# A recommender tower with a three-layer cross network: another opening order, and a later copy of the third chunk's x

## Chip, cores and metric

One core of a Trainium2 chip runs the whole program. The metric is device time in microseconds (us), the median over the runs of one kernel. TensorE is called PE here, VectorE DVE, ScalarE ACT, GpSimd POOL and SyncE SP, as in the profile.

## What is computed

A batch of 512 samples, each with 64 categorical fields. Every field's row (16 floats) is gathered from its table, the 64 x 16 block x goes through three layers of a cross network, and a small multi-layer perceptron follows.

```python
e = stack([tbl_f[ids[:, f]] for f in range(64)], axis=1)     # 512 x 64 x 16
h = x = e
outs = []
for W in (W0, W1, W2):                                       # W0: 64*64 x 128, W1, W2: 64*128 x 128
    h = einsum('bid,bjd,ijn->bnd', x, h, W)
    outs.append(h)
z = sum(concatenate(outs, axis=1), axis=-1)                  # 512 x 384
h = relu(concatenate([z, dense_ctx], 1) @ W_top1 + b_top1)
h = relu(h @ W_top2 + b_top2)
y = h @ W_top3
```

## The kernel before, in words

The 512 samples x 16 dimensions are 8192 columns, worked in 16 **chunks** of 512 columns (32 samples), t = 0 to 15. All five instruction streams are written out by hand with semaphores; each runs the function `chunk(bt, q, t)` once per chunk, chunk 0 with q = -1 and the others with q = 0 to 3 in four blocks. Inside a chunk the order is given by 64 **places** p: at each place PE fills one PSUM bank of a ring of four (`fill_bank`, L848: three 128x512 matmuls, L870 to L872, for four fields i of layer 1), and either ACT (`scale_bank`, L673, at the places of `A_IN`, 7 of each 16) or DVE (`take_bank`, L551, at the other 9) takes the bank, scaling it with x and summing. PE may fill place p only when place p - 4 has been taken (L861 to L867). POOL adds up what ACT has scaled (`add_pairs`, L434, lines L447 to L453) and closes each quarter of a chunk (`finish_block`, L455). ACT may write its y buffer again only when POOL has read it (L684).

While chunk t runs, the same streams prepare the next ones at fixed places. POOL gathers the table rows of chunk t + 2 (`gather`, L422, one indirect DMA per step), SP stores them to DRAM turned (L307), loads them as x (L330, tile `xx`) and in nine rotated groups (`load_roll`, L316, tile `roll`, a ring of four). ACT copies x into the PSUM tile `xx_ps` (`copy_xx`, L631). DVE multiplies every rotated group with `xx_ps` (`product`, L501, line L519), and PE contracts these products with W0 into `acc` (layer 0, L828, L812 to L817, L823). ACT and DVE round and split the result h1 for the next chunk (L657, L540). During chunk t DVE forms the products of chunk t + 1; from chunk 1 on the first of them stands at place 0, ahead of that place's bank. ACT's copy of the x of chunk t + 2 stands at place `XX_COPY_AT` = 56 of 64 of chunk t, in chunk 0 as in all others (L762).

**The opening.** Chunk 0 is cut into two halves of 256 columns, so that layer 1 can begin with the first.
- SP loads the first indices and row offsets (L332, L333), then the other chunks' (L334, L335). POOL adds them (L486) and gathers, 8 indirect DMAs for the first half and 8 for the second (L491), then 16 for chunk 1 (L429).
- ACT issues at once, waiting for nothing, W0 in four loads (L713 to L716), three constants (L718) and W1 in eight parts of 512 KB (L720); it rounds parts 0 to 3 (L724) and waits for the first x.
- SP waits for the first 8 gathers, stores the half twice (L313, tensor `x_halves`), waits for that, loads x (L339) and the nine rotated groups, two loads each (L327). Groups 4 to 8 wait until product g - 4 has freed their ring slot. After group 3 it waits for the second half's gathers and stores that half.
- ACT copies the first x to `xx_ps` (L729), the turned x to `xcol` (L731), rounds W1's parts 4 to 7 and the split part of W0 (`w0_hi`, L736).
- DVE sums W0 (L575 to L577), forms the low parts of W1 0 to 3 (`w1_rest`, L578, line L580), then the nine products of the first half with the other four `w1_rest` after products 1, 3, 5 and 7 (L585 to L588), then the split of h1 (L546, L548) and the low part of W0 (L591).
- PE runs `WARM` = 20 matmuls on W1's first part (L919), turns the first x (L844), does layer 0 of the first half (L925), and starts `fill_bank` of chunk 0 when h1 is rounded (L739) and split (L546). The second half's layer 0 stands at places 8 to 24 of chunk 0.

```python
for g in range(GROUPS):                                         # SP, L340
    if g >= ROLL:
        sp.wait_ge(first_prod_ready, g - ROLL + 1)
    load_roll(x_halves[0], g, (g - GROUPS) % ROLL, first_roll_loaded, HALVES[0])
    if g == ROLL - 1:
        sp.wait_ge(first_gathered[1], 16 * HALF_STEPS)
        store_half(1)
```

Of the kernel before, what the change touches and what calls it, by code (L numbers as in the profile page):

```python
# [5 lines left out]
F32 = mybir.dt.float32  # L6
# [3 lines left out]
ALU = mybir.AluOpType  # L10
# [31 lines left out]
GROUPS = 9  # L42
# [6 lines left out]
W1_PARTS = 8  # L49
# [28 lines left out]
WARM = 20  # L78
# [7 lines left out]
FIRST_STORE_AT, FIRST_XX_LOAD_AT = 48, 50  # L86
# [43 lines left out]
def build(nc, ins, out):  # L130
    with ExitStack() as ctx:
# [160 lines left out]
        def gathers(t):  # L292
            return not isinstance(t, int) or t + 2 < CHUNKS
# [7 lines left out]

        @block.sync
        def _(sp):
# [6 lines left out]
            def store_half(half):  # L310
                for copy in range(2):
                    dst = x_halves[half, copy * FIELDS:(copy + 1) * FIELDS, :]
                    sp.dma_start(dst.rearrange("(s f) (b d) -> (f b) s d", f=HALF_F, d=DIM),  # L313
                                 rows[:, 0, half * HALF_STEPS:(half + 1) * HALF_STEPS, :]).then_inc(first_stored[half], 16)

            def load_roll(x, g, slot, loaded, cols=slice(0, CH)):  # L316

                width = cols.stop - cols.start
                if g == WHOLE:
                    for part in (slice(0, FIELDS // 2), slice(FIELDS // 2, FIELDS)):  # L320
                        src = x[FIELDS // 2 + part.start:FIELDS // 2 + part.stop, :]
                        sp.dma_start(roll[part, slot, 0, cols], src).then_inc(loaded[slot], 16)
                    return
                for half in range(2):
                    first = x[4 * g + half:4 * g + half + 1, :]
                    src = bass.AP(first.tensor, first.offset, [[width, FIELDS], [2 * width, 2], [1, width]])
                    sp.dma_start(roll[half * FIELDS:(half + 1) * FIELDS, slot, :, cols], src).then_inc(loaded[slot], 16)  # L327
# [12 lines left out]
            for g in range(GROUPS):  # L340
                if g >= ROLL:
                    sp.wait_ge(first_prod_ready, g - ROLL + 1)
                load_roll(x_halves[0], g, (g - GROUPS) % ROLL, first_roll_loaded, HALVES[0])
                if g == ROLL - 1:
                    sp.wait_ge(first_gathered[1], 16 * HALF_STEPS)
                    store_half(1)
# [153 lines left out]
        def _(dve):  # L500
# [81 lines left out]

            for k in range(W1_PARTS // 2):
                w1_rest(k)
            for g in range(GROUPS):  # L585
                first_product(g)
                if g % 2 == 1:
                    w1_rest(W1_PARTS // 2 + g // 2)  # L588
            first_split_h1()
            dve.wait_ge(w0_hi_ready, 1)  # L590
            dve.tensor_tensor(w0_lo[:], w0_whole[:], w0_hi[:].bitcast(F32), ALU.subtract).then_inc(w0_lo_ready, 1)  # L591
# [38 lines left out]
        def _(act):  # L630
# [81 lines left out]
            act.sem_inc(z3_copied, 1)  # L712
            act.dma_start(w0[:], ins["w0_tiles"][:, 0:RAW_TILES, :]).then_inc(w0_loaded, 16)  # L713
# [5 lines left out]
            for k in range(W1_PARTS):  # L719
                act.dma_start(w1_whole[:, w1_parts[k]], ins["w1_rows"][:, w1_parts[k]]).then_inc(w1_loaded[k], 16)  # L720

# [3 lines left out]

            for k in range(W1_PARTS // 2):
                round_w1(k)
            act.wait_ge(first_xx_loaded, 16)
# [4 lines left out]
            for k in range(W1_PARTS // 2, W1_PARTS):  # L733
                round_w1(k)
            act.wait_ge(w0_summed, 1)
            act.activation(w0_hi[:], w0_whole[:], ACT.Copy).then_inc(w0_hi_ready, 1)  # L736
# [4 lines left out]
            def chunk(bt, q, t):  # L741
                last = is_last(t)
                for p in range(PLACES):
# [18 lines left out]
                    if p == XX_COPY_AT and gathers(t):  # L762
                        copy_xx(t + 2)
# [287 lines left out]
```

## Time and profile before

| what | value |
|---|---|
| median of 3 runs | 1139.14 us (1136.38 to 1140.77) |
| the profiled execution's own time | 1139.9 us |
| its span, first to last instruction | 1138.1 us |
| PE busy | 1100.9 us (97%) |
| DVE / ACT / POOL busy | 901.2 (79%) / 684.9 (60%) / 913.9 us (80%) |
| mean granted clock of PE | 0.99 |

The span is 1.8 us short of the execution's own time. The shares are means over the whole span: what a stage loses has to be read in the stage, by the waits and the order of time there. Times in the rows further down are us from the start of the span. In the timeline a row gives start, duration, engine, line, operation and tiles, a count, and in brackets the idle time of the engine before it with what ended it; "SPq" and "ACTq" are the issuing of DMAs by SP and ACT.

### The profile page before, as it was taken

The numbers are of one execution on the slowest core, as the hardware profiler recorded it, in microseconds if no ns is written. First come the engines' busy times: TensorE is split into PE (matmuls) and PEld (weight loads), VectorE is DVE, ScalarE is ACT, GpSimd is POOL, SyncE is SP. The second block draws the span as 40 slices with busy tenths as digits, with TensorE's granted clock in tenths as the row PEclk, the third lists the DMA queues.
The fourth block names the chain that finished last, engine by engine and source line by source line (L and its number), as shares of the span: only waits on it lengthen the run. The fifth ranks groups of instructions, "written<-read, shape, count | busy, mean of one in ns | idle before, by whom it ended". The sixth has DMA issues, their size and how long they took to land.

```text
span 1138.1 us, 17464 instructions
## 1 busy us (share of the span) xinstructions
PE 1100.9 (97%) x4802; PEld 818.8 (72%) x4802; DVE 901.2 (79%) x2567; ACT 684.9 (60%) x2132; POOL 913.9 (80%) x848
## 2 busy tenths in 40 slices
PE   2898999999999999999999999999999999999999
PEld 2666677777778777777678777777777777777775
DVE  2788788988887788888887698989887588988750
ACT  3354666666664566666665466766665466666751
POOL 6778798989989598898889689898988769966740
PEclk8899899999999999999999999999999999999999
DMA  7573514252444425243251634315153621523000
GB/s 267 132 182 66 140 34 112 46 119 57 94 119 103 104 45 113 64 92 85 39 134 48 164 82 85 87 18 140 28 131 82 164 63 29 129 79 127 1 1 1
DMA packets 128100, 102.51 MB, mean 90 GB/s; under 512 B 77569, under 2 KB 87041, under 8 KB 127490
## 3 DMA queue, kind: packets, MB, share of 16 engines
q1 hardware_dynamic: 117714, 92.89, 33.0%
q0 software_dynamic: 8192, 2.11, 2.2%
q10 hardware_dynamic: 2096, 6.40, 1.4%
q8 instruction: 38, 0.62, 0.2%
q14 instruction: 60, 0.49, 0.2%
HBM read 97.16 MB, written 4.20 MB: 89 GB/s over the span
## 4 chain that ended last, share of the span: by engine, by line
PE 80%; POOL 12%; DMA 3%; issue 2%; DVE 1%; ACT 1%; SPq 0%; POOLq 0%; ACTq 0%; DVEq 0%
PE tps L870 19%; PE tps L872 18%; PE tps L871 18%; PE acc L828 8%; POOL ysum_sb L450 5%; PE side L897 5%; POOL rows_sb L429 4%; PE side L884 3%; PE acc L812 2%; PE acc L817 2%; PE acc L813 2%; PE acc L823 1%; PE side L892 1%; PE tps L964 1%; POOL ysum_sb L447 1%
## 5 line engine op out<-in xcount | busy, mean ns | idle before, releaser
L688 ACT ACTIVATE y_sb<-tps,xcol_sb 128x128 f32<-128x128 f32 x1792 | 511.5, 375 | 365.2 <-PE tps L872 325.4
L571 DVE SCALAR_TENSOR_TENSOR parts_sb<-tps,xcol_sb,parts_sb 128x128 f32<-128x128 f32 x2176 | 604.9, 341 | 152.1 <-PE tps L872 150.4
L450 POOL TENSOR_TENSOR ysum_sb<-ysum_sb,y_sb 128x512 f32<-128x512 f32 x319 | 421.0, 1320 | 72.7 <-ACT y_sb L688 50.0
L870 PE MATMUL tps<-w_hi_sb,h_hi_sb 128*128 128x512 f32 x1024 | 464.8, 454 | 6.2 <-ACT y_sb L688 4.6
L871 PE MATMUL tps<-w_lo_sb,h_hi_sb 128*128 128x512 f32 x1024 | 405.9, 396 | 0.0
L872 PE MATMUL tps<-w_hi_sb,h_lo_sb 128*128 128x512 f32 x1024 | 405.9, 396 | 0.0
L429 POOL DMA_INDIRECT rows_sb<-tables,rows_now_sb x240 | 255.4, 1064 | 61.4 <-issue 25.5
L870 PEld LDWEIGHTS tps<-w_hi_sb,h_hi_sb 128*128 128x128 f32 x1024 | 193.4, 189 | 97.2 <-issue 25.7
L871 PEld LDWEIGHTS tps<-w_lo_sb,h_hi_sb 128*128 128x128 f32 x1024 | 193.8, 189 | 65.6 <-issue 28.8
L872 PEld LDWEIGHTS tps<-w_hi_sb,h_lo_sb 128*128 128x128 f32 x1024 | 193.4, 189 | 46.6
L519 DVE TENSOR_TENSOR prod_sb<-roll_sb,xx_ps 128x1024 f32<-128x1024 f32 (+1 forms) x136 | 155.9, 1146 | 14.1 <-DMA roll_sb<-x_halves 12.7
L828 PE MATMUL acc<-prod_sb,w_sb 128*128 128x512 f32 (+1 forms) x272 | 135.4, 585 | 4.5 <-DVE prod_sb L519 4.5
L447 POOL TENSOR_TENSOR ysum_sb<-y_sb 128x512 f32<-128x512 f32 x64 | 82.6, 1291 | 17.3 <-ACT y_sb L688 8.7
L533 DVE TENSOR_TENSOR lo_sb<-prod_sb,hi_sb 128x1024 fp32r<-128x1024 f32 x60 | 95.2, 1587 | 0.3
L652 ACT ACTIVATE hi_sb<-prod_sb 128x1024 fp32r<-128x1024 f32 x60 | 64.4, 1073 | 15.6 <-DVE prod_sb L519 15.6
L699 ACT ACTIVATE gsum_sb<-side 128x256 f32<-128x256 f32 x128 | 65.1, 691 | 3.7 <-PE side L884 3.7
L828 PEld LDWEIGHTS acc<-prod_sb,w_sb 128*128 128x128 f32 x272 | 49.8, 193 | 20.6 <-issue 7.4
L453 POOL TENSOR_TENSOR ysum_sb<-ysum_sb 128x256 f32<-128x256 f32 x63 | 51.0, 810 | 4.9
L460 POOL TENSOR_TENSOR ysum_sb<-ysum_sb,parts_sb 128x256 f32<-128x256 f32 x63 | 47.7, 757 | 5.9 <-DVE parts_sb L571 0.4
L812 PE MATMUL acc<-hi_sb,w_hi_sb 128*128 128x512 f32 x120 | 48.9, 408 | 0.0
L567 DVE TENSOR_SCALAR parts_sb<-tps,xcol_sb 128x128 f32<-128x128 f32 x128 | 38.5, 342 | 11.8 <-PE tps L872 11.0
L813 PE MATMUL acc<-hi_sb,w_lo_sb 128*128 128x512 f32 x120 | 47.2, 393 | 0.0
(72 smaller groups left out, 607.6 us busy)
## 6 DMA issues: line engine op xcount, KB each, us to landing
roll_sb<-x_scratch SPq DMA_DIRECT2D x240, 256.0 KB, 4.2
w_sb<-w_rows SPq DMA_DIRECT2D x40, 256.0 KB, 4.2
gsum_sb<-w_rows ACTq DMA_DIRECT2D x8, 512.0 KB, 8.9
roll_sb<-x_halves SPq DMA_DIRECT2D x32, 128.0 KB, 2.9
rows_sb<-tables,rows_now_sb POOLq DMA_INDIRECT x240
x_scratch<-rows_sb SPq DMA_DIRECT2D x30, 128.0 KB, 4.1
xx_sb<-x_scratch SPq DMA_DIRECT2D x15, 256.0 KB
roll_sb<-x_scratch SPq DMA_DIRECT2D x30, 64.0 KB, 1.9
```

Of the source, the lines that this page charges most:

```text
L429: pool.indirect_dma_start(rows[:, slot, s, :], None, ins["tables"], bass.IndirectOffsetOnAxis(ap=rows_now[:, s:s + 1].bitcast(U32), axis=0 ...
L447: pool.tensor_tensor(ysum[:], y[:, 0], y[:, 1], ALU.add).then_inc(y_step, 1)
L450: pool.tensor_tensor(ysum[:], ysum[:], y[:, bank], ALU.add).then_inc(y_step, 1)
L519: dve.tensor_tensor(prod[:, slot, :, cols], roll[:, ring, :, cols], xx_ps[:, :, cols].to_broadcast([P, 2, cols.stop - cols.start]), ALU.mu ...
L533: dve.tensor_tensor(lo[:, slot], prod[:, slot], hi[:].bitcast(F32), ALU.subtract).then_inc(lo_ready, 1)
L571: dve.scalar_tensor_tensor(part, bank, scale, part, ALU.mult, ALU.add).then_inc(d_done, 1)
L688: done = act.activation(y[:, bank, u * NF:(u + 1) * NF], tps[:, p % RING, u * NF:(u + 1) * NF], ACT.Copy, scale=xcol[:, (q + 1) % 2, s, i: ...
L812: pe.matmul(acc[:], w0_hi[:, 2 * e + i, :], hi[:, i, :], start=False, stop=False, skip_group_check=True)
L828: mm = pe.matmul(acc[:, cols], weights, prod[:, slot, i, cols], start=g == 0 and i == 0, stop=False, skip_group_check=True)
L870: pe.matmul(bank, h1_hi[:, par, cols], w1_hi[:, of], start=True, stop=False, skip_group_check=True)
L871: pe.matmul(bank, h1_hi[:, par, cols], w1_lo[:, of], start=False, stop=False, skip_group_check=True)
L872: pe.matmul(bank, h1_lo[:, par, cols], w1_hi[:, of], start=False, stop=True, skip_group_check=True).then_inc(t_ready, 1)
```

## The change

- ACT waits for the first indices (`first_ids_loaded`) before it issues its loads of W0, constants and W1, and issues only the first four parts of W1 then.
- ACT rounds the split part of W0 right after W1's parts 0 to 3, and DVE forms its low part right after `w1_rest(3)`, ahead of the first product.
- When the first half is stored, ACT issues the second half-load of the rotated groups 0 to 3, then W1's parts 4 to 7, and then copies x and the turned x. SP issues x, the first half-load of groups 0 to 3 and both of groups 4 to 8.
- SP's store of the second half moves from after group 3 to after group 8.
- DVE's `w1_rest` of parts 4 and 5 stand after products 4 and 6, those of parts 6 and 7 after the split of h1.
- `WARM` is 26 in place of 20.
- In chunk 0 alone, ACT's copy of chunk 2's x stands at place 63 in place of 56.

```diff
--- before.py
+++ after.py
@@ -46,7 +46,8 @@
 RAW = tuple(g for g in range(WHOLE) if g not in SPLIT)
 SPLIT_TILES, RAW_TILES = 2 * len(SPLIT), 2 * len(RAW)
 ROLL = 4
-W1_PARTS = 8
+W1_PARTS, W1_EARLY = 8, 4
+W1_BEHIND = (4, 6)
 W2_I, W2_SLOTS = 4, 4
 F_SETS = FIELDS // W2_I
 W2_KEPT = 4
@@ -75,7 +76,7 @@
 HALVES = (slice(0, HALF), slice(HALF, CH))
 HALF_F = P // (SAMPLES // 2)
 HALF_STEPS = FIELDS // HALF_F
-WARM = 20
+WARM = 26
 LATE_XX_AT, LATE_XCOL_AT = 4, 6
 LATE_PROD_AT = tuple(range(6, 6 + 2 * GROUPS, 2))
 LATE_L0_AT = tuple(p + 2 for p in LATE_PROD_AT)
@@ -83,7 +84,7 @@
 FIRST_L0_AT = tuple(range(32, 32 + 3 * GROUPS, 3))
 FIRST_ROLL_AT = (30, 33, 36, 39, 42)
 FIRST_GATHER_AT = tuple(range(16, 16 + 2 * STEPS, 2))
-FIRST_STORE_AT, FIRST_XX_LOAD_AT = 48, 50
+FIRST_STORE_AT, FIRST_XX_LOAD_AT, FIRST_XX_COPY_AT = 48, 50, PLACES - 1
 FIRST_NEXT_ROLL_AT = (51, 52, 53, 54)
 
 
@@ -299,6 +300,23 @@
 
             return (GROUPS * (q + 2) + g) % size
 
+        def load_roll_half(eng, x, g, half, slot, loaded, cols):
+
+            width = cols.stop - cols.start
+            if g == WHOLE:
+                part = slice(half * FIELDS // 2, (half + 1) * FIELDS // 2)
+                src = x[FIELDS // 2 + part.start:FIELDS // 2 + part.stop, :]
+                eng.dma_start(roll[part, slot, 0, cols], src).then_inc(loaded[slot], 16)
+                return
+            first = x[4 * g + half:4 * g + half + 1, :]
+            src = bass.AP(first.tensor, first.offset, [[width, FIELDS], [2 * width, 2], [1, width]])
+            eng.dma_start(roll[half * FIELDS:(half + 1) * FIELDS, slot, :, cols], src).then_inc(loaded[slot], 16)
+
+        def load_first_roll(eng, g, half):
+            if g >= ROLL:
+                eng.wait_ge(first_prod_ready, g - ROLL + 1)
+            load_roll_half(eng, x_halves[0], g, half, (g - GROUPS) % ROLL, first_roll_loaded, HALVES[0])
+
         @block.sync
         def _(sp):
             def store_rows(t, slot, steps, stored):
@@ -314,17 +332,8 @@
                                  rows[:, 0, half * HALF_STEPS:(half + 1) * HALF_STEPS, :]).then_inc(first_stored[half], 16)
 
             def load_roll(x, g, slot, loaded, cols=slice(0, CH)):
-
-                width = cols.stop - cols.start
-                if g == WHOLE:
-                    for part in (slice(0, FIELDS // 2), slice(FIELDS // 2, FIELDS)):
-                        src = x[FIELDS // 2 + part.start:FIELDS // 2 + part.stop, :]
-                        sp.dma_start(roll[part, slot, 0, cols], src).then_inc(loaded[slot], 16)
-                    return
                 for half in range(2):
-                    first = x[4 * g + half:4 * g + half + 1, :]
-                    src = bass.AP(first.tensor, first.offset, [[width, FIELDS], [2 * width, 2], [1, width]])
-                    sp.dma_start(roll[half * FIELDS:(half + 1) * FIELDS, slot, :, cols], src).then_inc(loaded[slot], 16)
+                    load_roll_half(sp, x, g, half, slot, loaded, cols)
 
             def load_xx(t):
                 sp.dma_start(xx[:], x_of(t)).then_inc(xx_loaded, 16)
@@ -338,12 +347,10 @@
             sp.wait_ge(first_stored[0], 32)
             sp.dma_start(xx[:, HALVES[0]], x_halves[0]).then_inc(first_xx_loaded, 16)
             for g in range(GROUPS):
-                if g >= ROLL:
-                    sp.wait_ge(first_prod_ready, g - ROLL + 1)
-                load_roll(x_halves[0], g, (g - GROUPS) % ROLL, first_roll_loaded, HALVES[0])
-                if g == ROLL - 1:
-                    sp.wait_ge(first_gathered[1], 16 * HALF_STEPS)
-                    store_half(1)
+                for half in range(1 if g < ROLL else 2):
+                    load_first_roll(sp, g, half)
+            sp.wait_ge(first_gathered[1], 16 * HALF_STEPS)
+            store_half(1)
             sp.wait_ge(first_stored[1], 32)
             sp.dma_start(xx[:, HALVES[1]], x_halves[1]).then_inc(xx_loaded, 16)
             for g in range(GROUPS):
@@ -580,15 +587,17 @@
                 dve.tensor_tensor(w1_lo[:, w1_parts[k]], w1_whole[:, w1_parts[k]], w1_hi[:, w1_parts[k]].bitcast(F32),
                                   ALU.subtract).then_inc(w1_lo_ready, 1)
 
-            for k in range(W1_PARTS // 2):
+            for k in range(W1_EARLY):
                 w1_rest(k)
+            dve.wait_ge(w0_hi_ready, 1)
+            dve.tensor_tensor(w0_lo[:], w0_whole[:], w0_hi[:].bitcast(F32), ALU.subtract).then_inc(w0_lo_ready, 1)
             for g in range(GROUPS):
                 first_product(g)
-                if g % 2 == 1:
-                    w1_rest(W1_PARTS // 2 + g // 2)
+                if g in W1_BEHIND:
+                    w1_rest(W1_EARLY + W1_BEHIND.index(g))
             first_split_h1()
-            dve.wait_ge(w0_hi_ready, 1)
-            dve.tensor_tensor(w0_lo[:], w0_whole[:], w0_hi[:].bitcast(F32), ALU.subtract).then_inc(w0_lo_ready, 1)
+            for k in range(W1_EARLY + len(W1_BEHIND), W1_PARTS):
+                w1_rest(k)
 
             def chunk(bt, q, t):
                 at = product_at(q)
@@ -710,30 +719,42 @@
                 act.activation(z[:, 2, bass.ds(bt * P, P)], side[:, 0, 0:P], ACT.Copy).then_inc(z3_copied, 1)
 
             act.sem_inc(z3_copied, 1)
+
+            act.wait_ge(first_ids_loaded, 32)
             act.dma_start(w0[:], ins["w0_tiles"][:, 0:RAW_TILES, :]).then_inc(w0_loaded, 16)
             act.dma_start(w0_whole[:], ins["w0_tiles"][:, RAW_TILES:TILES0, :]).then_inc(w0_loaded, 16)
             act.dma_start(w0_back[:], ins["w0_back"]).then_inc(w0_loaded, 16)
             act.dma_start(w0_end[:], ins["w0_end"]).then_inc(w0_loaded, 16)
             for dst, src in ((ident, "identity"), (mask, "sample_mask"), (mask8, "sum_mask")):
                 act.dma_start(dst[:], ins[src]).then_inc(consts_loaded, 16)
-            for k in range(W1_PARTS):
+
+            def load_w1(k):
                 act.dma_start(w1_whole[:, w1_parts[k]], ins["w1_rows"][:, w1_parts[k]]).then_inc(w1_loaded[k], 16)
+
+            for k in range(W1_EARLY):
+                load_w1(k)
 
             def round_w1(k):
                 act.wait_ge(w1_loaded[k], 16)
                 act.activation(w1_hi[:, w1_parts[k]], w1_whole[:, w1_parts[k]], ACT.Copy).then_inc(w1_hi_ready, 1)
 
-            for k in range(W1_PARTS // 2):
+            for k in range(W1_EARLY):
                 round_w1(k)
+            act.wait_ge(w0_summed, 1)
+            act.activation(w0_hi[:], w0_whole[:], ACT.Copy).then_inc(w0_hi_ready, 1)
+            act.wait_ge(first_stored[0], 32)
+            for g in range(ROLL):
+                load_first_roll(act, g, 1)
+
+            for k in range(W1_EARLY, W1_PARTS):
+                load_w1(k)
             act.wait_ge(first_xx_loaded, 16)
             act.activation(xx_ps[:, 0, HALVES[0]], xx[:, HALVES[0]], ACT.Copy).then_inc(first_xx_copied, 1)
             act.wait_ge(first_xcol_filled, 1)
             act.activation(xcol[:, 0, 0:SUB // 2], side[:, 1, 0:SUB // 2 * FIELDS].rearrange("p (s f) -> p s f", f=FIELDS),
                            ACT.Copy).then_inc(first_xcol, 1)
-            for k in range(W1_PARTS // 2, W1_PARTS):
+            for k in range(W1_EARLY, W1_PARTS):
                 round_w1(k)
-            act.wait_ge(w0_summed, 1)
-            act.activation(w0_hi[:], w0_whole[:], ACT.Copy).then_inc(w0_hi_ready, 1)
             act.wait_ge(consts_loaded, 48)
             act.wait_ge(first_prod_used, GROUPS)
             act.activation(h1_hi[:, 0, HALVES[0]], acc[:, HALVES[0]], ACT.Copy).then_inc(first_h1_hi, 1)
@@ -759,7 +780,7 @@
                             round_h1(q, t + 1)
                     if p in XDIAG_AT:
                         diagonal(q, t, XDIAG_AT.index(p))
-                    if p == XX_COPY_AT and gathers(t):
+                    if p == (FIRST_XX_COPY_AT if q < 0 else XX_COPY_AT) and gathers(t):
                         copy_xx(t + 2)
                     if q >= 0:
                         if p - 2 in G_AT:
```

## Rows read from the trace of the kernel before

**Rows 1.** PE waits of the whole span: engine line, waited for, total us, times, longest

```profile
PE tps L870 <- ACT y_sb L688: 4.6, 1, 4.6
```

**Rows 2.** Timeline, end of chunk 0: PE, ACT, POOL

```profile
107.86 0.50 PE L870 MATMUL tps<-w_hi_sb,h_hi_sb 128*128 128x512 f32 x1
...
113.84 0.60 ACT L639 ACTIVATE xx_ps<-xx_sb 128x512 f32<-128x512 f32 x1 [7.58 <-DMA xx_sb<-x_scratch]
...
115.58 1.28 POOL L450 TENSOR_TENSOR ysum_sb<-ysum_sb,y_sb 128x512 f32<-128x512 f32 x1 [3.76 <-ACT y_sb L688]
...
123.15 0.22 POOL L424 TENSOR_TENSOR rows_now_sb<-ids_sb,table_rows_sb 128x16 int32<-128x16 int32 x1
```

**Rows 3.** Busy time in two stretches: length, engines, PEclk, DMA share, GB/s

```profile
5.00:17.00 12.00, 5.20 (x15) 4.19 (x16) 7.25 (x7) 5.51 (x5) 8.92 (x9) 1.00 1.03 406
115.50:121.30 5.80, 5.74 (x14) 4.48 (x15) 3.67 (x11) 3.81 (x14) 4.06 (x4) 0.50 1.06 239
```

**Rows 4.** Chain of waits, opening: start, us, what

```profile
1.22 3.64 DMA first_table_rows_sb<-first_table_rows
...
6.10 1.09 POOL rows_sb L491
...
16.73 3.31 DMA rows_sb<-tables,first_rows_sb
...
20.48 2.65 DMA x_halves<-rows_sb
```

**Rows 5.** Timeline, opening: ACT, SP, DVE and PE

```profile
0.83 0.39 ACTq L713 DMA_DIRECT2D w_sb<-w_tiles  x1
...
4.50 3.96 ACTq L720 DMA_DIRECT2D gsum_sb<-w_rows  x8
...
14.48 1.06 ACT L724 ACTIVATE w_hi_sb<-gsum_sb 128x1024 fp32r<-128x1024 f32 x1 [0.24 <-DMA gsum_sb<-w_rows]
...
23.53 5.21 SPq L327 DMA_DIRECT2D roll_sb<-x_halves  x8
...
25.20 0.39 ACT L729 ACTIVATE xx_ps<-xx_sb 128x256 f32<-128x256 f32 x1 [9.66 <-DMA xx_sb<-x_halves]
...
30.82 5.14 SPq L327 DMA_DIRECT2D roll_sb<-x_halves  x8
...
34.19 0.69 DVE L519 TENSOR_TENSOR prod_sb<-roll_sb,xx_ps 128x512 f32<-128x512 f32 x1 [0.59 <-DMA roll_sb<-x_halves]
...
41.23 0.38 ACT L739 ACTIVATE h_hi_sb<-acc 128x256 fp32r<-128x256 f32 x1 [10.44 <-PE acc L823]
...
42.32 1.22 DVE L591 TENSOR_TENSOR w_lo_sb<-w_whole_sb,w_hi_sb 128x1024 fp32r<-128x1024 f32 x1
...
43.45 0.60 DVE L567 TENSOR_SCALAR parts_sb<-tps,xcol_sb 128x128 f32<-128x128 f32 x2
...
46.59 0.39 PE L870 MATMUL tps<-w_hi_sb,h_hi_sb 128*128 128x512 f32 x1
```

**Rows 6.** DMA issues: tiles, queue, count, KB each, median us from issue to landing

```profile
roll_sb<-x_halves SPq DMA_DIRECT2D x32, 128.0 KB, 2.9
...
xx_sb<-x_halves SPq DMA_DIRECT2D x2, 128.0 KB, 2.0
ids_sb<-ids_steps SPq DMA_DIRECT2D x1, 128.0 KB, 6.0
...
first_ids_sb<-first_ids SPq DMA_DIRECT2D x1, 8.0 KB, 2.5
```

**Rows 7.** Chain of waits, end of chunk 0

```profile
111.36 2.46 DMA xx_sb<-x_scratch
```

**Rows 8.** Timeline, chunk 3: POOL, ACT and PE

```profile
295.85 1.29 POOL L447 TENSOR_TENSOR ysum_sb<-y_sb 128x512 f32<-128x512 f32 x1
...
297.18 1.14 ACT L688 ACTIVATE y_sb<-tps,xcol_sb 128x128 f32<-128x128 f32 x4 [2.00 <-POOL ysum_sb L447]
...
299.98 0.39 PE L870 MATMUL tps<-w_hi_sb,h_hi_sb 128*128 128x512 f32 x1
```

## The prediction, made before the changed kernel ran

> **What bounds the kernel.** I read the waits of PE first. PE is 97% busy over the span and DVE, ACT and POOL are not, so what can be won is time in which PE stands or runs slowly. In the 1,000 us of chunks 1 to 15 there is next to none of that; two places are left, and the change touches both.
>
> The first is the end of chunk 0: one wait of 4.6 us for a bank that ACT had not taken [rows 1]. The timeline says why. ACT stood for 7.58 us at place 56 for the x of chunk 2, which a DMA still brought, and the scaling of place 56 is queued behind that copy; PE filled places 56 to 59 and then had no bank left [rows 2]. After the wait PE ran 5.80 us at a granted clock of 0.50 (1.2 of 2.4 GHz), 14 matmuls [rows 3]. So the stall is paid twice.
>
> The second is the opening. The chain of waits there runs: row offsets by DMA, gathers on POOL, the last gather's landing, the store of the half [rows 4], then the rotated groups and their products. The reader should see in the timeline that product 4 waited for its rotated group (34.19), which SP had issued only at 30.82, and that h1 is rounded at 41.23, from where PE's stream starts [rows 5].
>
> **The change, part by part.** The sum is made against the profiled execution, 1139.9 us (span 1138.1); it lies 0.8 us above the median of 1139.14.
>
> **Indices first.** ACT's first load was issued at 0.83 and now waits for the indices. The row offsets landed 3.64 us after their issue at 1.22, beside ACT's stream [rows 4]; the other small load, issued when that stream had just begun, took 2.5 [rows 6]. I take 2.5: indices at 3.7, 1.15 earlier (bounds 0 and 1.6, the latter from the 2.0 of the x load). ACT's loads all move 2.9 us later. What hides that: part 3 of W1 is rounded at 14.48 + 1.06 + 2.9 = 18.4 and the split part of W0 one rounding later at 19.5, before the first half is stored. The low part of W0 costs DVE its 1.22 us [rows 5] before the first product, while DVE waits anyway.
>
> **Gathers.** The first starts at 6.10 - 1.15 = 4.95, the eighth started 10.63 later [rows 4]. In that stretch the DMA engines were full (share 1.03, 406 GB/s) [rows 3]; with ACT's stream 2.9 us later, more gathers run before it, and I take another 1.2 us off the slow ones (bounds 0 and 2.1). The eighth starts at 14.4, lands 3.31 later at 17.7, and the store (0.4 of issue, 2.65) ends at 20.8 in place of 23.1: 2.3 us earlier.
>
> **ACT's queue after the store.** It now issues four half-loads of rotated groups at 5.21/8 = 0.65 and four W1 parts at 3.96/8 = 0.50 before the copy of x: 4.6 us [rows 5]. So x is copied at 25.4, where it was copied at 25.20: that 2.3 us is spent again, and queued behind it are the copy of the turned x and W1's rounding. But the groups have landed by then, and the first product starts at 25.8 and ends at 26.5.
>
> **Groups 4 to 8.** SP is free (its issues are halved and the second store stands behind), so group 4 is issued at 26.5 in place of 30.82. Before, product 4 began 3.37 after that issue [rows 5], so 29.85 if nothing is in the way. In the way are W1's parts 4 to 7, issued at 23.4 to 25.4: 2.1 MB at the 406 GB/s of rows 3 take 5.2 us, after the 2.0 us that x took to land [rows 6], until 30.6. Group 4 lies between 29.85 and 31.2 (its 256 KB behind all of them); I take 30.6, nearer the full stretch, since a 128 KB load beside ACT's stream took 6.0 us where x took 2.0 [rows 6]. Product 4 gains 3.6 us.
>
> On this the Trainium skill ("DMA: Bandwidth & Descriptors", section "Queues, rings and completion order") says that each DMA engine takes turns between the queues at packet boundaries. By that rule the group would not stand behind all of W1 but share with it, which I estimate at 0.6 us of delay, and the result would be 0.1 to 0.2 us lower.
>
> **From product 4 to h1.** It took 41.23 - 34.19 = 7.04 us with two `w1_rest` among the products; it has two again (after products 4 and 6). So h1 is rounded at 37.6, **3.6 us earlier**. Bounds: 5.6 earlier (gathers 1.3 better, group 4 undisturbed), 1.1 later (gathers no earlier, group 4 like the 6.0 us load). The other edits here I cost at nothing: six more warm-up matmuls end before x lands at 23, and if x came first only the turned x, which waits behind ACT's copy, would be late. The second half is stored at about 33.4 and its x lands near 39, while its copy stands at 47.81 - 3.6. After the split of h1 DVE now has two `w1_rest` (2.44) where it had one subtraction of 1.22 [rows 5], so its first bank moves from 43.45 to 44.67 (before the shift) and is done by 45.8; PE needs that bank at 46.59 [rows 5], so 0.8 us of cover is left.
>
> **The copy at place 63.** All that follows shifts by 3.6, so I stay in the times of before. ACT takes place 56 when PE has filled it, at 107.86 + 0.9, and is through with 56, the rounding of h1 and places 58, 60, 62 at about 114.1. The x landed at 111.36 + 2.46 = 113.8 [rows 7], because its chain hangs on SP's store of chunk 1, which hangs on PE's stream and shifts with it. So ACT copies without waiting, until 114.7. Queued behind the copy is ACT's place 65, and waiting for it is DVE's first product of chunk 2, for which DVE is free at 115.1. PE loses some 0.2 us at place 63. Gone are 4.64 of waiting and, of the 5.80 us at half clock, 14 matmuls' excess over the full-clock pitch of 0.23: 5.80 - 3.26 = 2.5. Net **-7.0** (bounds -7.3, and -5.0 if x is 2 us later against the stream).
>
> **POOL's slack.** POOL stood 3.76 us in that stall too and used it to catch up. Without it, four additions of 1.28 with their gaps and the closing one run from 111.8 to 118.5, where the next gather's index sum began at 123.15 [rows 2]: POOL gains 4.65 and PE 7.0, so POOL is 2.35 closer to being late. The tightest place I found in the first block is in chunk 3: ACT's first bank of the last quarter began at 297.18, right when POOL's addition (295.85 + 1.29) freed its buffer [rows 8]. It would be some 2.3 late; PE needs that bank at 299.98 and had it at 298.3, so 1.7 is covered and **+0.7** is left (bounds 0 and 2.3).
>
> **Sum:** 1139.9 - 3.6 - 7.0 + 0.7 = 1130.0, or 1129.3 in terms of the median.
>
> **Rivals.**
> - *POOL sets the pace* (0.10): PE gets back only what POOL gets. For it: the slack of nearly nothing in chunk 3. Against it: PE showed no wait there, and the last chunk of a block refills the slack. Then -3.6 - 4.65: 1130.9 in the median's terms, and more if DVE's wait for POOL's result adds to it, to 1132.
> - *The opening gives nothing* (0.17): the 4.6 us in ACT's queue and W1's stream eat the earlier gathers. For it: x is copied no earlier. Then -7.0 + 0.7: 1132.8.
> - *The wait only moves* (0.10): x of chunk 2 comes later against the stream, and DVE's product holds up the bank of place 64 behind it. It decides from 0.4 us of lateness on, 1:1; at 3 us with some time at the low clock after it, about 4 us come back: 1133 to 1134.
> - *Slower than before* (0.03): DVE's queue is in order, and `w1_rest` of part 4 stands ahead of products 5 to 8. Every us that part 4 lands after about 30 is a us on h1. The gain is gone when it lands near 40, over 16 us after its issue; above that the kernel is slower, 1140 to 1143. Against it: four parts take 5.2 us at the rate of rows 3.
>
> **How the numbers follow.** The forecast has 0.60. The range takes in its bounds (1126 to 1134 with the terms not all at one end) and the second and third rivals: 1125.5 to 1135.0. About 0.5% (5.7 us, so 1133.4) is what a measurement of this kernel tells from no change. Faster: 0.60 + 0.10, most of the second rival's 0.17 and a little of the third's 0.10, so 0.82; slower 0.03; the same 0.15.
>
> **What would show it.** Right: ACT's copy of chunk 2's x without a wait, no wait of PE for ACT near 107 and full clock there; the first gather near 5; product 4 near 30.6; h1 rounded near 37.6; small PE waits around 293. Wrong: DVE waiting for `xx_ps` or group 4 for long, h1 at 40 or later, or a pause of PE at place 68 of about the old length.

## The result, and the profile after

| | before | after |
|---|---|---|
| median of 18 runs each, on the same chip | 1137.53 us (1135.39 to 1140.77) | 1135.12 us (1129.59 to 1139.14) |
| ratio, with its 95% interval | | 0.9975 (0.9965 to 0.9985) |
| the profiled execution | 1139.9 us (span 1138.1) | 1132.33 us (span 1130.5) |

The change gains 2.8 us (0.25% of 1137.53; 1.7 to 4.0). That is clear of no change, but under the 0.5% that I had taken as the least that counts. I had forecast 10 us and a range that ended at 1135.0. The opening is where the forecast fails. The chain of waits of the changed kernel, which answers to [rows 4] (start, us, what):

```profile
1.22 1.83 DMA first_table_rows_sb<-first_table_rows
...
4.28 1.09 POOL rows_sb L498
...
13.57 3.43 DMA rows_sb<-tables,first_rows_sb
...
17.44 2.83 DMA x_halves<-rows_sb
...
27.25 8.63 DMA roll_sb<-x_halves
```

The indices, the gathers and the store came 2.8 us earlier than in [rows 4] (stored at 20.3 where it was 23.1), half a us better than forecast. Then group 4 took 8.63 us to land. The timeline shows what that did, and, further down, the end of chunk 0 (against [rows 5] and [rows 2]):

```profile
20.29 2.62 ACTq L313 DMA_DIRECT2D roll_sb<-x_halves  x4
...
22.95 2.42 ACTq L732 DMA_DIRECT2D gsum_sb<-w_rows  x4
...
25.42 0.39 ACT L752 ACTIVATE xx_ps<-xx_sb 128x256 f32<-128x256 f32 x1 [6.72 <-issue]
...
28.90 0.69 DVE L526 TENSOR_TENSOR prod_sb<-roll_sb,xx_ps 128x512 f32<-128x512 f32 x1 [1.70 <-PE acc L849]
...
29.73 1.06 ACT L739 ACTIVATE w_hi_sb<-gsum_sb 128x1024 fp32r<-128x1024 f32 x1 [3.73 <-DMA gsum_sb<-w_rows]
...
30.61 0.69 DVE L526 TENSOR_TENSOR prod_sb<-roll_sb,xx_ps 128x512 f32<-128x512 f32 x1 [1.02 <-PE acc L849]
...
35.70 1.06 ACT L739 ACTIVATE w_hi_sb<-gsum_sb 128x1024 fp32r<-128x1024 f32 x1 [1.72 <-DMA gsum_sb<-w_rows]
...
35.90 0.69 DVE L526 TENSOR_TENSOR prod_sb<-roll_sb,xx_ps 128x512 f32<-128x512 f32 x1 [4.61 <-DMA roll_sb<-x_halves]
...
43.20 0.38 ACT L760 ACTIVATE h_hi_sb<-acc 128x256 fp32r<-128x256 f32 x1 [6.44 <-PE acc L844]
...
46.56 0.60 DVE L574 TENSOR_SCALAR parts_sb<-tps,xcol_sb 128x128 f32<-128x128 f32 x2
...
47.82 0.47 PE L891 MATMUL tps<-w_hi_sb,h_hi_sb 128*128 128x512 f32 x1 [0.64 <-DVE parts_sb L578]
...
115.50 0.60 ACT L648 ACTIVATE xx_ps<-xx_sb 128x512 f32<-128x512 f32 x1
...
117.99 0.73 PEld L905 LDWEIGHTS side<-xdiag_sb,h2t_sb 64*128 64x128 f32 x8 [0.36 <-issue]
...
118.38 1.22 DVE L526 TENSOR_TENSOR prod_sb<-roll_sb,xx_ps 128x1024 f32<-128x1024 f32 x1 [1.95 <-DMA roll_sb<-x_scratch]
...
120.69 0.50 PE L891 MATMUL tps<-w_hi_sb,h_hi_sb 128*128 128x512 f32 x1 [1.57 <-DVE parts_sb L578]
```

The reader is to see six things. x is copied at 25.42, as forecast. Products 2 and 3, at 28.90 and 30.61, wait for PE to finish layer 0 of an earlier group. Product 4 starts at 35.90 where 30.6 was forecast, behind a wait for its group. h1 is rounded at 43.20, 2 us later than in [rows 5] and not 3.6 earlier. PE's first stop for DVE is at 47.82, behind the two `w1_rest` that now stand after the split of h1. At the end of chunk 0 ACT copies x without a wait, but DVE then waits 1.95 us for a rotated group, with the bank of place 64 queued behind it. The waits of PE (total, times, longest) show that the 4.6 us for ACT of [rows 1] are gone and that waits for products and for DVE's banks take their place:

```profile
PE acc L849 <- DVE prod_sb L526: 9.4, 4, 4.2
...
PE tps L891 <- DVE parts_sb L578: 2.2, 2, 1.6
```

Before, PE waited for products too, but for half as long, and had no such wait for DVE's banks:

```profile
PE acc L828 <- DVE prod_sb L519: 4.6, 5, 2.2
```

The DMA view of 26 to 32 us says who had the engines (q1 is SP's queue with the rotated groups, q10 ACT's with W1; packets, which are mostly single rows of a load, MB, share of 16 engines):

```profile
DMA packets 886, 2.23 MB, mean 371 GB/s; under 512 B 130, under 2 KB 404, under 8 KB 886
...
q10 hardware_dynamic: 565, 2.00, 91.1%
q1 hardware_dynamic: 206, 0.19, 10.5%
```

Three marks are used below to compare kernels: **h1**, the start of the rounding of the first half, and **marks 1 and 2**, the starts of the first two `form_g` of the program (PE's `side<-xdiag_sb,h2t_sb`, early in chunk 1 and a quarter of that chunk later: 123.99 and 139.55 in the profile predicted from, 15.56 apart; 117.99 and 135.19 after). Each is read from one profiled execution. What follows mark 2 took between 997.1 and 1002.0 us in the twelve profiles (the execution's time less mark 2): it differs mainly in three places where PE waits for rows of W2 (0 to 2.2 us each) and in the tail after chunk 15 (42.0 or 43.7 us). So a mark tells of its stretch, and only the median over the runs tells of the time.

### The profile page after: what moved, and what is told of

It reads as the page before. It is cut to its first block, busy times and chain, and to the rows that moved or that the text cites. A ratio compares the mean times of both kernels' runs of the same rounds, so it can differ in the third digit from the quotient of the medians.

```text
span 1130.5 us, 17476 instructions
## 1 busy us (share of the span) xinstructions
PE 1096.4 (97%) x4808; PEld 815.6 (72%) x4808; DVE 896.7 (79%) x2567; ACT 684.9 (61%) x2132; POOL 911.8 (81%) x848
## 4 chain that ended last, share of the span: by engine, by line
PE 89%; POOL 4%; DMA 4%; DVE 2%; issue 1%; ACT 1%; ACTq 0%; SPq 0%; POOLq 0%; DVEq 0%
PE tps L891 21%; PE tps L893 20%; PE tps L892 20%; PE acc L849 9%; PE side L918 5%; PE side L905 3%; PE acc L833 2%; PE acc L838 2%; PE acc L834 2%; POOL rows_sb L436 1%; PE acc L844 1%; PE side L913 1%; POOL ysum_sb L457 1%; PE tps L985 1%; DMA roll_sb<-x_halves 1%
## 5 line engine op out<-in xcount | busy, mean ns | idle before, releaser
L436 POOL DMA_INDIRECT rows_sb<-tables,rows_now_sb x240 | 253.4, 1056 | 61.6 <-issue 25.5
L540 DVE TENSOR_TENSOR lo_sb<-prod_sb,hi_sb 128x1024 fp32r<-128x1024 f32 x60 | 90.1, 1501 | 0.3
```

The source lines that it names most:

```text
L436: pool.indirect_dma_start(rows[:, slot, s, :], None, ins["tables"], bass.IndirectOffsetOnAxis(ap=rows_now[:, s:s + 1].bitcast(U32), axis=0 ...
L540: dve.tensor_tensor(lo[:, slot], prod[:, slot], hi[:].bitcast(F32), ALU.subtract).then_inc(lo_ready, 1)
```

## The experiments

| run | median us (runs) | ratio to before | h1 | marks 1, 2 |
|---|---|---|---|---|
| copy_alone | 1133.16 (6) | 0.9959 (0.9944 to 0.9973) | 41.17 | 115.03, 135.40 |
| opening_alone | 1140.84 (10) | 1.0029 (1.0019 to 1.0040) | 42.22 | 123.71, 139.27 |
| w1_all_early | 1132.42 (12) | 0.9953 (0.9937 to 0.9968) | 40.56 | 115.26, 135.62 |
| product_later | 1133.26 (6) | 0.9967 (0.9953 to 0.9980) | 42.78 | 117.52, 133.07 |
| x_ahead | 1135.95 (12) | 0.9988 (0.9975 to 1.0002) | 43.94 | 118.11, 137.20 |
| warm_behind | 1133.66 (6) | 0.9955 (0.9940 to 0.9969) | 38.97 | 113.85, 135.34 |
| copy_product | 1132.56 (5) | 0.9956 (0.9942 to 0.9970) | 41.69 | 115.64, 131.20 |
| before_look | 1136.02 (1) | | 41.54 | 121.16, 136.71 |
| w1_short_rows | 1133.72 (5) | 0.9962 (0.9948 to 0.9977) | 41.26 | 116.00, 136.34 |
| best | 1128.92 (5) | 0.9930 (0.9915 to 0.9944) | 38.26 | 113.04, 128.59 |

Each ratio is to runs of before on the same chip (medians 1138.03, 1137.28 and 1137.55 in the three groups of runs). Us below are a ratio's distance from 1, times 1137.5.

**The two halves of the change.** copy_alone is the kernel before with one edit; opening_alone is the changed kernel without it.

```diff
-FIRST_STORE_AT, FIRST_XX_LOAD_AT = 48, 50
+FIRST_STORE_AT, FIRST_XX_LOAD_AT, FIRST_XX_COPY_AT = 48, 50, PLACES - 1
...
-                    if p == XX_COPY_AT and gathers(t):
+                    if p == (FIRST_XX_COPY_AT if q < 0 else XX_COPY_AT) and gathers(t):
```

> The kernel before with ACT's copy of chunk 2's x at place 63 of chunk 0, nothing else. Theory A (the two halves of the change are independent, and DVE's first product of chunk 2 then waits for its rotated group): PE's wait of 4.6 us for ACT and the low clock behind it are gone, a wait of 1 to 2 us at place 68 takes their place, and the time is 5 to 6 us below before. Rival B (POOL sets the pace once the stall is gone): 2 to 4 us below, with PE waits in chunks 2 and 3. Rival C (the copy only gains together with the new opening): within 1.5 us of before.

> The changed kernel with ACT's copy of chunk 2's x back at place 56. Theory A (W1's second half holds up the rotated groups 4 to 8): product 4 near 36, h1 rounded near 43, and 1 to 3 us slower than before, since the stall at place 60 is back at its old length. Rival D (the opening gains and the copy does not): 2 to 4 us below before.

The copy alone gains 4.7 us, a little under theory A's 5 to 6; the opening alone loses 3.3 (2.2 to 4.6), a little over theory A's 1 to 3. The marks agree on the opening: h1 lies at 41.17 to 41.69 in the four profiles with the old opening (before, before_look, copy_alone, copy_product) and at 42.22 to 43.20 in the three with the new one (after, opening_alone, product_later). Timeline of copy_alone at the end of chunk 0:

```profile
112.50 0.62 ACT L639 ACTIVATE xx_ps<-xx_sb 128x512 f32<-128x512 f32 x1
...
116.74 1.22 DVE L519 TENSOR_TENSOR prod_sb<-roll_sb,xx_ps 128x1024 f32<-128x1024 f32 x1 [3.28 <-DMA roll_sb<-x_scratch]
...
119.05 0.50 PE L870 MATMUL tps<-w_hi_sb,h_hi_sb 128*128 128x512 f32 x1 [2.89 <-DVE parts_sb L571]
```

ACT stands for nothing, as forecast; DVE does, 3.28 us, not for x but for rotated group 0 of chunk 2, which SP issues behind x. PE then stood 2.89 us, longer than theory A's 1 to 2, and ran at the lower clock behind it (columns as in [rows 3]), where it stayed at 1.00 behind the 1.57 us of after:

```profile
120.00:122.00 2.00, 2.00 (x6) 1.54 (x5) 1.91 (x6) 0.54 (x3) 1.78 (x3) 0.50 1.05 234
```

The timeline of opening_alone shows group 4 late again, h1 late, and the old stall in its old place:

```profile
34.96 0.69 DVE L526 TENSOR_TENSOR prod_sb<-roll_sb,xx_ps 128x512 f32<-128x512 f32 x1 [3.64 <-DMA roll_sb<-x_halves]
...
42.22 0.38 ACT L760 ACTIVATE h_hi_sb<-acc 128x256 fp32r<-128x256 f32 x1 [6.44 <-PE acc L844]
...
115.45 0.80 PE L891 MATMUL tps<-w_hi_sb,h_hi_sb 128*128 128x512 f32 x1 [4.76 <-ACT y_sb L697]
```

**What holds up group 4.** w1_all_early is the changed kernel with all eight parts of W1 issued in the first stream.

```diff
-            for k in range(W1_EARLY):
+            for k in range(W1_PARTS):
                 load_w1(k)
...
-            for k in range(W1_EARLY, W1_PARTS):
-                load_w1(k)
```

> The changed kernel with all eight parts of W1 issued where the first four are, so that nothing of W1 is in flight beside the rotated groups. Theory A: the loads of group 4 take 3 to 4 us in place of 8.6, product 4 starts at 30 to 32, h1 is rounded at 37 to 39.5 (43.2 in the changed kernel), and the time is 3.5 to 5 us below the changed kernel's. Rival E (the groups are late because of the gathers beside them or the split over two queues, not of W1): group 4 still takes 6 us or more and h1 stays at 42 or later. Rival F (W1's stream then slows the gathers and the store as it did before): the first half is stored at 22.5 or later (20.3 in the changed kernel) and half of the gain is lost.

No half-load of a rotated group took more than 4.1 us now (7.9 after), so the second half of W1 was what held up group 4, as theory A has it. Product 4 no longer waits for its group but for PE's layer 0:

```profile
33.84 0.69 DVE L526 TENSOR_TENSOR prod_sb<-roll_sb,xx_ps 128x512 f32<-128x512 f32 x1 [1.02 <-PE acc L847]
```

That is 2.1 us earlier than after, and still later than theory A's 30 to 32; h1 at 40.56 and a time 2.5 us below the changed kernel's fall short of it too. Rival F came with it. The price stands in its chain, beside W1's stream: the last gather lands in 5.48 us and the store takes 3.81 (3.43 and 2.83 after), 3 us in all. x is copied only 0.8 later all the same (26.21), since ACT has no W1 to issue ahead of it; the first product starts 1.5 later (27.45).

x_ahead keeps W1's second half late, but issues it behind ACT's copies of x and the turned x.

```diff
             for g in range(ROLL):
                 load_first_roll(act, g, 1)
-            for k in range(W1_EARLY, W1_PARTS):
-                load_w1(k)
...
+            for k in range(W1_EARLY, W1_PARTS):
+                load_w1(k)
             for k in range(W1_EARLY, W1_PARTS):
                 round_w1(k)
```

> The changed kernel with ACT's copies of x and of the turned x ahead of its four issues of W1's second half, which come some 1 us later for it. Theory A (group 4 is late by as much of W1's second half as is queued before it): the first product starts near 23.5 in place of 25.9, group 4 is issued 2.4 us earlier, ahead of most of W1, and lands at 29 to 32 (35.9 in the changed kernel); h1 is rounded 2 to 4 us earlier, and the time is 2 to 3 us below the changed kernel's. Rival H (W1's stream takes the engines whenever it comes, and groups 4 to 7 then end with it): product 4 or 5 still at 35 or later, and the time within 1 us of the changed kernel.

Its timeline:

```profile
23.72 1.80 ACTq L732 DMA_DIRECT2D gsum_sb<-w_rows  x4
23.82 0.69 DVE L526 TENSOR_TENSOR prod_sb<-roll_sb,xx_ps 128x512 f32<-128x512 f32 x1 [3.11 <-DMA roll_sb<-x_halves]
...
36.68 0.69 DVE L526 TENSOR_TENSOR prod_sb<-roll_sb,xx_ps 128x512 f32<-128x512 f32 x1 [7.00 <-DMA roll_sb<-x_halves]
```

The first product is 2.1 us earlier than after, and product 4 is 0.8 later: theory A fails, and the times of rival H come. Copying x sooner does not help while group 4 stands against W1. By the ratios the time is 1.5 us above the changed kernel's, which the intervals cannot tell from none. The DMA view of 26 to 32 us of x_ahead:

```profile
DMA packets 842, 2.08 MB, mean 347 GB/s; under 512 B 119, under 2 KB 398, under 8 KB 842
...
q10 hardware_dynamic: 508, 1.83, 84.5%
q1 hardware_dynamic: 246, 0.23, 12.0%
```

w1_short_rows is x_ahead with the same bytes in rows of 1 KB, eight transfers in place of four (parts 4 and 5, and 6 and 7, wait together).

```diff
-            for k in range(W1_EARLY, W1_PARTS):
-                load_w1(k)
+            for k in range(W1_EARLY, W1_PARTS, 2):
+                for j in range(4):
+                    at = slice(w1_parts[k].start, w1_parts[k + 1].stop)
+                    dst, src = (x.rearrange("p (a n) -> p a n", a=2)[:, :, j * 256:(j + 1) * 256]
+                                for x in (w1_whole[:, at], ins["w1_rows"][:, at]))
+                    act.dma_start(dst, src).then_inc(w1_loaded[k], 16)
```

> The run with x copied ahead of the second half of W1 again, but that half goes in eight transfers of 1 KB rows (256 KB each) where it went in four of 4 KB rows (512 KB each): the same bytes, on the same queue, with as large a row as the turned groups have. Theory J (the engines that move the data give each queue a turn by packets, and a packet of 4 KB against one of 1 KB is why SyncE's queue got a tenth of the bytes from 26 to 32 us): with equal packets SyncE's queue carries a third to a half of the bytes while W1 moves, group 4 has landed 3 us earlier than in the run with 4 KB rows (first product of group 4 at 33 to 34.5, there 36.68), h_hi 40.5 to 42. Theory K (the queue that was served first is served until it is empty, whatever its packets): SyncE's queue again gets under a fifth of the bytes, group 4 at 36 or later. In both the rounding of W1 parts 4 to 7 begins later by the four further issues (some 2.4 us). Time: J 1132 to 1135, K 1135 to 1138.

The DMA view of the same stretch:

```profile
DMA packets 1937, 1.79 MB, mean 298 GB/s; under 512 B 171, under 2 KB 1937, under 8 KB 1937
...
q10 hardware_dynamic: 1437, 1.39, 77.7%
q1 hardware_dynamic: 413, 0.38, 23.1%
```

Its product 4:

```profile
32.71 0.69 DVE L526 TENSOR_TENSOR prod_sb<-roll_sb,xx_ps 128x512 f32<-128x512 f32 x1 [3.13 <-DMA roll_sb<-x_halves]
```

Product 4 began 4.0 us earlier than in x_ahead, and h1 at 41.26: as early as theory J has them, or earlier. Its share does not come: SP's queue had 21% of the bytes here (0.38 of 1.79 MB) and 11% there, not a third. Nor is the row size all that differs: ACT's eight issues last until 28.4 us, where x_ahead's four were out at 25.5, so that less of W1 was issued ahead of group 4. This run does not part the two.

By packets SP's queue had 23% of them after (206 of 886), 29% in x_ahead, 21% here. But these are means over a stretch in which the share changes. In the changed kernel both loads of group 4 had been issued by 27.9 us, and yet from 28 to 30 us SP's queue moved next to nothing:

```profile
q10 hardware_dynamic: 214, 0.79, 100.4%
...
q1 hardware_dynamic: 2, 0.00, 0.2%
```

Later the two queues moved about as many packets each, and the bytes went with the row size. From 30 to 32 us of x_ahead:

```profile
q10 hardware_dynamic: 155, 0.57, 79.6%
q1 hardware_dynamic: 144, 0.13, 21.0%
```

With short rows the share swings as well: SP's queue had 58 of 641 packets from 27 to 29 us, 161 of 646 from 30 to 32, and 669 of 1425 from 32 to 36. So there is no fixed share, by bytes or by packets. Why SP's queue gets next to none at first stays open.

**What bounds the opening once W1 is out of the way.** warm_behind is w1_all_early with ten more warm matmuls and six more behind the turned x.

```diff
-WARM = 26
+WARM, WARM_BEHIND = 36, 6
...
+            for k in range(WARM_BEHIND):
+                pe.matmul(tps[:, k % RING, :], w1_hi[:, 0:P], w1_hi[:, 0:CH], start=True, stop=True)
```

> The kernel with all of W1 issued early, with 36 warm-up matmuls in place of 26 and 6 more behind the turned x, so that PE does not stand between the warm-up and layer 0. There product 4 waited for layer 0 of the groups before it, at a granted clock of 0.50. Theory I (the clock is the next bound of the opening): the granted clock is 1.00 from 26 to 34, a group's layer 0 takes 1.0 to 1.1 us in place of 1.7 to 2.0, product 4 starts 1.5 to 2.3 us earlier and h1 is rounded 1 to 2 us earlier. Rival J (the loads of groups 4 to 8 are right behind it): h1 moves by less than 0.5 us, with DVE waiting for roll instead of PE.

Busy time in two stretches of w1_all_early, and then of warm_behind (columns as in [rows 3]):

```profile
26.00:30.00 4.00, 2.03 (x6) 1.66 (x7) 1.29 (x2) 3.79 (x6) 2.57 (x5) 0.67 0.89 232
30.00:34.00 4.00, 4.00 (x11) 3.10 (x11) 1.53 (x3) 0.57 (x1) 3.08 (x4) 0.50 0.68 178
```

```profile
26.00:30.00 4.00, 3.50 (x15) 2.34 (x16) 1.96 (x3) 3.74 (x6) 2.57 (x5) 1.00 0.85 246
30.00:34.00 4.00, 3.65 (x15) 2.26 (x13) 2.99 (x5) 0.62 (x1) 3.08 (x4) 1.00 0.77 199
```

At the lower level (0.50, 1.2 GHz) PE was full from 30 to 34 us with 11 matmuls, so layer 0 set the pace; at 1.00 it did 15, product 4 began 2.0 us earlier (31.80), h1 came 1.6 us earlier and mark 1 1.4 earlier, as theory I has it. Yet the time is no better, and mark 2 shows where the gain goes: it lies at 135.34, as in copy_alone (135.40), w1_all_early (135.62) and after (135.19), whose first marks differ by 4 us. PE stopped 3.51 us at place 68 for DVE, and DVE 3.90 us for group 0 of chunk 2. By and large the wait is longer where the first mark is earlier (1.57 us in after, 3.51 here), and all these kernels but after run at the lower clock behind it. x_ahead and w1_short_rows, which have the wait too, lie at 137.20 and 136.34.

**The wait at place 68.** product_later is the changed kernel, copy_product is copy_alone, each with DVE's first product of chunk 2 at place 4 in place of 0, behind the first banks of chunk 1.

```diff
-                at = product_at(q)
+                at = product_at(q) if t != 1 else (4,) + product_at(q)[1:]
```

> The changed kernel with DVE's first product of chunk 2 at place 4 of chunk 1 in place of 0, behind two banks. Theory A (PE's 1.6 us at place 68 is DVE standing for rotated group 0 ahead of the bank of place 64): that wait is gone and the time is 1 to 1.6 us below the changed kernel's. Rival G (the wait moves to layer 0's first matmul at place 8 or to the next product): no gain, and a PE wait of the same length for the product.

> The kernel before with the copy of chunk 2's x at place 63, and DVE's first product of chunk 2 at place 4 of chunk 1. With the copy alone PE stood 2.9 us at place 68 behind DVE's wait for rotated group 0, and ran some 4 us at half clock after it. Theory A: both are gone, no PE wait over 1 us between 100 and 130, the second stage gains 7 us against before in the profile, and the time is 2 to 4 us below the copy alone, 6.5 to 8 below before. Rival G (the wait for the group moves to layer 0 at place 8): the time stays within 1 us of the copy alone.

In both the view of PE's waits is empty from 100 to 130 us, and the marks are 15.55 and 15.56 apart, as before; with the product at place 0 they are 17.2 (after) and 20.37 (copy_alone). So theory A is right about the waits in both runs. In time little of this can be told from none: product_later lies 0.9 us under the changed kernel, and copy_product is as good as level with copy_alone (0.3 us), within the intervals, where 2 to 4 us were expected. Its mark 2 lies 4.2 us ahead of copy_alone's; why the medians do not show that is open. The marks are of one execution each, and copy_alone's was the slowest of its six (1136.02).

**The kernel before, in a second profile.**

> The kernel before once more, for a second profile of it. If the opening of the first profile is typical, h1 is rounded within 0.5 us of 41.2 and form_g of chunk 1 comes within 0.5 us of 124.0; what differs from the first profile then lies in the waits for W2 (0 to 2 us) and in the tail after chunk 15, which took 43.7 us in four of six profiles so far and 42.0 in two. If not, the opening itself varies, and the two stages have to be compared over several profiles.

The start of chunk 0's stream in the profile that I predicted from, and then in this one (columns as in [rows 3]):

```profile
42.90:46.40 3.50, 3.50 (x10) 2.69 (x10) 2.30 (x8) 1.14 (x4) 2.89 (x3) 0.51 0.32 83
```

```profile
42.90:46.40 3.50, 3.50 (x17) 2.82 (x16) 3.23 (x10) 1.99 (x8) 2.89 (x3) 1.00 0.41 100
```

The same kernel, 10 matmuls in one execution and 17 in the other: mark 1 lies 2.83 us apart. Behind the stall, too, the low level lasted 5.80 us in the one [rows 3] and 2.9 in the other (114.1 to 117.0 at 0.51, 1.00 after it). The 2.83 us hold both.

**All of it together.** best is warm_behind with the product at place 4 (both diffs above).

> The change, and three edits that the runs so far pointed to: all of W1 issued before the turned x is stored, six more warm matmuls behind the turn, and DVE's first product of chunk 2 moved from place 0 to place 4. If the parts add: h_hi at 39.0 as in the run with warm matmuls behind (42.2 to 43.2 with the change), no wait of TensorE over 1.3 us from 100 to 130 us, where the run with warm matmuls behind waited 3.5, and a start of chunk 1's gathers 2.5 us ahead of the run with the copy and the product alone; 1128 to 1130.5. Rival (what is won in the opening is lost further on, in the waits for W2's rows or for GpSimd in chunks 1 to 4): within 1 us of the run with copy and product alone, 1131.5 to 1133.5.

All of it came, or better: h1 at 38.26, mark 1 2.6 us ahead of copy_product, the marks 15.55 apart, no wait of PE from 100 to 130. 1128.92 is 8.0 us under before (6.4 to 9.7) and beats both kernels. Timeline of best: the product waits less than 1 us where it now stands.

```profile
38.26 0.38 ACT L758 ACTIVATE h_hi_sb<-acc 128x256 fp32r<-128x256 f32 x1 [7.79 <-PE acc L842]
...
114.32 1.22 DVE L526 TENSOR_TENSOR prod_sb<-roll_sb,xx_ps 128x1024 f32<-128x1024 f32 x1 [0.75 <-DMA roll_sb<-x_scratch]
```

## Why the prediction was wrong

- **Indices, gathers, store: right.** Forecast 3.7, 4.95 and 20.8; measured 3.05, 4.28 and 20.29. The indices moved by 1.8 us, a little beyond the upper bound of 1.6.
- **ACT's queue: right.** x at 25.4, measured 25.42. x_ahead shows that the 2.4 us of W1 issues in it did not matter in the end.
- **Group 4: the step that failed.** I let W1's second half move from 25.4 at the 406 GB/s of [rows 3] until 30.6, and group 4 in another 0.65 us at most behind it. Product 4 began at 35.90, far outside the bounds (29.85 to 31.2). The order was right and the end of W1 was not. Until 26 us ACT's queue moved 0.53 MB, its four half-loads of rotated groups (0.52 MB, issued ahead of W1, whose bytes I had left out), and then 2.00 MB by 32; the last landing signal of W1 came at 35.68, beside groups 4 to 7, which moved 0.88 MB from 32 to 36 us at 253 GB/s for all queues, with the engines full. Group 4 had next to nothing until 30 us. Of its 32 landing signals (16 for each load) 30 had come by 34.06, and the last, for which product 4 waits, at 35.88; products 5 and 6 follow without a wait for theirs. That W1 is the cause w1_all_early shows. That its row size is a part w1_short_rows makes likely; it does not show how much.
- **Layer 0's pace: a term that I had put at nothing.** I timed product 4 by its group alone. In the changed kernel products 2 and 3 waited for PE, which ran at a granted clock of 0.50 from 26 to 30 us, and came 1.7 us apart. PE was through with product 2's layer 0 at 31.5, so product 4 could not have begun before that with its group there. So some 1 of its 5.3 us of delay is layer 0's, hidden behind the group. w1_all_early, with the group there, shows this pace bare (product 4 at 33.84, 1.7 us behind product 3), and warm_behind takes it away (31.80).
- **The rule I weighed against it fails by its size.** Even sharing, from the Trainium skill's "DMA: Bandwidth & Descriptors", section "Queues, rings and completion order", gave 0.6 us of delay; the load's delay was 5. A packet of W1 carried up to four times the bytes of one of a group, and from 28 to 30 us SP's queue had 2 packets of 262, which no even sharing gives; where the packets were about even (x_ahead, 30 to 32 us), the trace agrees with turns.
- **The opening's sum:** -3.6 forecast, +3.3 measured on its own. "The opening gives nothing" (0.17) was the nearest rival and still too kind. Its opposite sign comes from group 4, from layer 0's pace and from one more step: the two `w1_rest` behind the split of h1, costed at nothing with 0.8 us of cover left. That cover was read from a stretch at the lower clock [rows 5]. With PE at full clock the bank was needed sooner: 0.70 us of wait in opening_alone at 46.90, where before_look has none. With h1 1.0 us later than in [rows 5] that is 1.7 of the 3.3; where the rest goes is not shown, since mark 1 of opening_alone lies 2.6 us behind before_look's and 0.3 ahead of the other profile's.
- **The copy at place 63: right in its mechanism, too large by a third.** -6.3 with POOL's share, -4.7 measured. The 4.6 us of waiting went. The 2.5 us at the lower clock were those of one execution: by before_look's 2.9 us with 7 matmuls they would be 2.90 - 7 x 0.23 = 1.3. And a new wait came, 2.89 in copy_alone, with some 2 us lost to the lower clock behind it (its marks are 20.37 apart, 4.8 over the usual 15.56): the rival "the wait only moves" (0.10) had the place and the queue right and the tile wrong, group 0 of chunk 2 and not x. I had given the moment when DVE is free for that product, and not asked when its group lands.
- **POOL's slack: not seen.** After has no wait of PE for it from 280 to 310 us, the place of the +0.7. "POOL sets the pace" falls.
- **"Slower than before" by part 4: no.** Part 4 was rounded at 29.73. The opening was slower on its own, but by the group and not by `w1_rest`.
- **Why the sum came out at -2.8** and not at 3.3 - 4.7 = -1.4: the intervals allow either. The marks give one reason for less than the sum: up to mark 1 after is 3 us behind copy_alone, and the wait at place 68 then takes 1.6 us from the one and 4.8 from the other, so that mark 2 is the same.

## What to carry to other kernels

Before a large load is moved next to a small urgent one, count all bytes that both queues have under way there, at the rate that each kind of load has shown, and expect the queue that comes later with short rows to get next to nothing at first. Here it helped to issue the large load earlier, at the price of 3 us in the gathers and the store; to copy x ahead of it did not. When a stall is taken away, ask of every operand of the next instruction in that queue, not only of the one that was late, when it lands, and of every engine how fast it works through what is queued before; a mark some us behind shows whether the gain is kept. Read the clock of a stretch in a second execution before its price or its slack goes into a sum.

## What was not expected of the hardware

- Two queues side by side have no fixed share. SP's had 2 of 262 packets from 28 to 30 us beside ACT's stream in after, and 144 of 334 from 30 to 32 in x_ahead; in after it moved 0.19 MB in the 6 us in which ACT's moved 2.00 MB.
- The 16 landing signals of one load can lie far apart on busy queues: 32.01 to 35.68 for W1's last part in after, where those of part 3, in the first stream, lie between 16.05 and 16.67.
- Full DMA engines are no fixed rate: 371 GB/s with W1's 4 KB rows from 26 to 32 us, 253 with the groups' 1 KB rows from 32 to 36. The Trainium skill's "Perfetto Trace Analysis", section "DMA Optimizations", says that transfers under 2 KB cost overhead and larger ones can raise throughput; read as rows, the trace agrees where W1 itself went in 1 KB rows (298 GB/s in w1_short_rows, 26 to 32 us). But the row is not all of it: the rotated groups of chunk 2, in 2 KB rows, ran at 239 GB/s with the engines as full [rows 3].
- The granted clock at the same place of the same kernel differs from run to run: 0.51 or 1.00 at the start of chunk 0's stream, and 2.9 or 5.8 us at about 0.50 after a stall of 4.6 to 5.1 us, together worth 2.8 us by mark 1.
